# Four records instead of eight in the granule of an edge sort that scatters with accumulating DMAs

## The chip, the cores and the metric

The kernel is one program on one core of a Trainium2 chip. Its time is the device time of one execution, in microseconds (us). Of the kernel before there are three runs, 4865.23, 4868.08 and 4868.71 us, with a median of 4868.08 us. The engines are called PE (TensorE), DVE (VectorE), ACT (ScalarE), POOL (GpSimd) and SP (SyncE, which only issues transfers here).

## The reference, cut to what matters

A graph of 12,500 nodes with 256 features and 200,000 weighted edges goes through a normalised graph convolution, a linear-attention mixer and a mixture of experts. The part that matters here is the convolution's sum over the edges of each source row:

```python
xn = _layernorm(x, axis=-1)
deg = segment_sum(ew_sl, row_sl, N);  dinv = rsqrt(deg)
norm = dinv[row_sl] * ew_sl * dinv[col_sl]
msgs = (xn @ W)[col_sl] * norm[:, None]
h7 = segment_sum(msgs, row_sl, N) + b        # row_sl = src, col_sl = dst, with self-loops
x = x + mlp(h7) + mixer(xn)
x = x + ffn(layernorm(x))                    # 8 experts, top 2
```

The source of an edge is drawn uniformly, and the edges come in the order of their destinations. So the kernel first sorts them on the chip by block of 128 source rows.

## The kernel before, in words

The nodes are cut into `BLOCKS` = 98 blocks of 128 rows. The edges lie as 128 partitions by 1568 columns, and are worked through in `LOTS` = 56 lots of `LOT` = 28 columns, 3584 edges each. The program runs in phases with a barrier behind each: `setup` (constants, a histogram of blocks by lot, the places where each block's tiles start), `sort_edges` (this is where the change acts), `degrees_and_rows`, `scale_table`, `gather_and_mix`, and then the node and expert phases.

`sort_edges` writes every edge as a record of two words (8 bytes) to its place in DRAM. Records are not written one by one but in granules: `GRANULE` = 8 consecutive records, 64 bytes. Within a lot, the edges of a block form a run. A run is shifted and padded so that it begins and ends on a granule's border of the final layout. A granule that a run fills only in part holds zeros in its other records, and since the scatter adds to zeroed DRAM, lots that share a granule complete each other. Two copies of the records in DRAM (`records0`, `records1`) take the even and the odd lots, and are added up in the next phase.

How many granules a lot may need is fixed when the program is built:

```python
GROUPS_OUT = -(-(LOT * P + BLOCKS * 2 * (GRANULE - 1)) // (GRANULE * P))
SLOTS_OUT = GROUPS_OUT * GRANULE
```

That is `GROUPS_OUT` = 5 groups of 128 granules, one granule for each partition, and `SLOTS_OUT` = 40 records for each partition. One lot `n` with buffer `h` (0 or 1) does this:

- DVE, L208 (`same_block`): compares blocks, for the ranks of lot n + 1. PE, L799 and L802: turns these into ranks in PSUM. DVE, L731 and L735 to L746 (`positions`): reduces them to a place for each edge and splits the place into lane (L737, the partition), group and record within the granule.
- DVE, L750, L755 and L762 (`routes`): one-hot matrices by lane and by slot, and six products of the slot matrix with the pieces of the record's values. ACT, L711 and L716: the doubled pieces, and the comparison that says which granules lie behind each run (128 x `GROUPS_OUT`*128 elements).
- PE, L811: one small matmul for each group, which makes the shift of each granule. PE, L820: 28 matmuls that put the records into their lanes and slots.
- DVE, L769, L772 and L774 (`leave`): the granules' addresses and the finished records `sort_rec`. L772 waits until the scatters of lot n - 2, which used the same buffer, have landed.
- POOL, L696: one indirect DMA for each group, `GROUPS_OUT` in all, that adds 128 granules to DRAM at the addresses `sort_addr`; granules with an address out of bounds are dropped.

The lines of the scatter, and of the wait for its landing:

```python
pool.wait_ge(rec_done, n + 1 + ONE); pool.wait_ge(addr_done, n + 1)
for g in range(GROUPS_OUT):                                            # L694
    pool.indirect_dma_start(
        out=k.granules[h], out_offset=bass.IndirectOffsetOnAxis(addr[:, h, g:g + 1], 0),
        in_=rec[:, h, g * GRANULE:(g + 1) * GRANULE, :], ..., compute_op=ALU.add).then_inc(scattered[h], 16)
```

```python
start_after(dve, scattered[h], SCATTERS * i)                           # SCATTERS = 16 * GROUPS_OUT
dve.tensor_tensor(addr[:, h, :], moved[:, :], s.granule_col, ALU.add).then_inc(addr_done, 1)   # L772
```

The order in which each engine works through this is written out in the code: DVE takes L208, `routes`, `positions` of the next lot, `leave`; PE takes the ranks of the next lot, L811, L820. No scheduler moves anything.

Of the kernel before, what the change touches and what calls it, by code (L numbers as in the profile page):

```python
# [35 lines left out]

assert TILES >= N_EDGES // P + BLOCKS
DST_BITS = 14
GRANULE_BITS = 3
GRANULE = 1 << GRANULE_BITS  # L40
LOT = 28
LOTS = EDGE_COLS // LOT
# [171 lines left out]
def setup(k, s):  # L214
    nc, A = k.nc, k.A
    with ExitStack() as ctx:
# [86 lines left out]
        with nc.Block() as block:  # L303
# [107 lines left out]
            def _(dve):  # L411
# [63 lines left out]
                dve.tensor_scalar(odd_i[:, :], ahead_i[:, :], GRANULE - 1, None, ALU.bitwise_and).then_inc(offs, 1)  # L475
                dve.tensor_scalar(quarter_i[:, :], ahead_i[:, :], GRANULE_BITS, None, ALU.arith_shift_right).then_inc(offs, 1)
                dve.tensor_scalar(tiles[:, :], tiles_i[:, :], 1.0, None, ALU.max).then_inc(offs, 1)
# [5 lines left out]
                dve.wait_ge(offs, 12)  # L483
                dve.tensor_scalar(run4_i[:, :], run3_i[:, :], GRANULE_BITS, None, ALU.arith_shift_right).then_inc(offs, 1)
                dve.wait_ge(offs, 13)
# [154 lines left out]
def sort_edges(k, s):  # L640
# [3 lines left out]
    with ctx:  # L644
# [43 lines left out]
        with nc.Block() as block:  # L688
# [32 lines left out]
            def _(dve):  # L721
# [5 lines left out]
                def positions(n):  # L727
                    for g in range(RANK_BANKS):
# [7 lines left out]
                    dve.wait_ge(q_done, n + 1)  # L736
                    dve.tensor_scalar(lane_i[:, :], q_i[:, :], GRANULE_BITS, P - 1, ALU.arith_shift_right,  # L737
                                      ALU.bitwise_and).then_inc(split_done, 1)
                    dve.tensor_scalar(high_i[:, :], q_i[:, :], 7 + GRANULE_BITS, GRANULE_BITS, ALU.arith_shift_right,
                                      ALU.logical_shift_left).then_inc(split_done, 1)  # L740
# [1660 lines left out]
```

## Time and profile before

| | |
|---|---|
| median of three runs | 4868.08 us |
| the profiled execution | 4868.08 us, its span 4866.3 us |
| `sort_edges`, first to last scatter | 171.4 to 930.5 us of the span |
| scatters (L696) | 280, 489.3 us busy, mean 1748 ns |
| granted clock of PE in that stretch | 0.62 of full speed |

The span runs from the first to the last instruction; 1.8 us of the profiled time lie around it. The profile gives for each engine how long it was busy, for each group of instructions what its idle time before them waited for, and a timeline by engine. Whether an engine matters is read in the stretch in question. In the page's strip of 40 slices, each of 121.7 us, slices 2 to 8 are the sort. A call of POOL for an indirect DMA is a busy instruction there: it is the time in which POOL makes the descriptors, not that of the transfer.

### The profile page before, as it was taken

To read this page: it belongs to the slowest core of one execution; us is meant where nothing else is said; L and a number is where in the kernel's file an instruction comes from. 1 tells how busy PE (TensorE), PEld (TensorE's weight loads), DVE (VectorE), ACT (ScalarE), POOL (GpSimd) and SP (SyncE) were. 2 spreads that over 40 slices of the span, in tenths; PEclk is the share of its full clock that TensorE was granted. 3 is DMA by queue.
4 is the path that set the end of the run, shared out by engine and by line. 5 is a ranking of instruction groups with operands and counts; after the bars stand their busy time and mean duration, and the time that the engine had idled before them with its cause. 6 is when DMAs were issued, how large, how long until landed. Compare 5 with 4: busy or idle time off the path is not lost. (4 is left out here: it accounts for less than half of the span.)

```text
span 4866.3 us, 90967 instructions
## 1 busy us (share of the span) xinstructions
PE 3803.9 (78%) x20723; PEld 2690.7 (55%) x20723; DVE 3267.5 (67%) x8693; ACT 1133.3 (23%) x3013; POOL 2642.9 (54%) x2385
## 2 busy tenths in 40 slices
PE   7688888487588888888777777777599689999970
PEld 6344444266344444444454445454288579999970
DVE  8899999688566666666666666665244855556643
ACT  2000000033211111111000000000055545555530
POOL 0366666400577777777777777777300022236656
PEclk9566666655799999999889888887599899999985
DMA  2011111133633333333444444444732012223344
GB/s 72 2 3 3 3 3 3 34 111 100 188 112 112 112 112 111 113 111 113 127 135 135 137 134 137 135 137 123 128 95 93 22 55 69 71 81 106 105 147 140
DMA packets 330249, 453.67 MB, mean 93 GB/s; under 512 B 96328, under 2 KB 260680, under 8 KB 330185
## 3 DMA queue, kind: packets, MB, share of 16 engines
q0 software_dynamic: 139776, 273.68, 23.0%
q1 hardware_dynamic: 175513, 169.50, 10.8%
q10 hardware_dynamic: 14898, 9.77, 0.7%
q8 instruction: 25, 0.41, 0.0%
q14 instruction: 37, 0.30, 0.0%
HBM read 354.82 MB, written 98.26 MB: 93 GB/s over the span
## 5 line engine op out<-in xcount | busy, mean ns | idle before, releaser
L1309 POOL DMA_INDIRECT rows<-table,idx x1664 | 1692.0, 1017 | 507.8 <-issue 288.0
L1593 PE MATMUL ps_seg<-rows,pick 128*128 128x256 f32 x3328 | 1150.0, 448 | 470.3 <-DMA rows<-table,idx 375.6
L1495 DVE TENSOR_TENSOR acc<-acc,ps_seg 128x256 f32 x1664 | 698.7, 420 | 718.6 <-PE ps_seg L1593 576.5
L1593 PEld LDWEIGHTS ps_seg<-rows,pick 128*128 128x128 f32 x3328 | 586.6, 206 | 959.0 <-DMA rows<-table,idx 464.1
L696 POOL DMA_INDIRECT records<-sort_rec,sort_addr x280 | 489.3, 1748 | 435.3 <-DVE sort_rec L774 349.5
L1374 DVE TENSOR_SCALAR pick<-iota_row,loc,ewt 128x128 f32<-128x128 f32 x1680 | 540.5, 360 | 21.3 <-DVE loc L1370 21.2
L2129 POOL DMA_INDIRECT arena<-ffn_rows,idx x212 | 215.4, 1016 | 454.6 <-DVE idx L2215 298.2
L2273 PE MATMUL ps_h<-arena,up_now 128*128 128x128 f32 x3392 | 415.8, 276 | 0.0
L2257 PE MATMUL ps_y<-down_now,arena 128*128 128x256 f32 x1696 | 401.0, 379 | 0.0
L2273 PEld LDWEIGHTS ps_h<-arena,up_now 128*128 128x128 f32 x3392 | 398.0, 193 | 0.1
L2257 PEld LDWEIGHTS ps_y<-down_now,arena 128*128 128x128 f32 x1696 | 306.1, 190 | 32.8
L820 PE MATMUL ps_out<-acc 128*128 128x240 bf16 x1568 | 277.7, 362 | 34.4 <-DVE acc L762 32.4
L2182 ACT ACTIVATE arena<-ps_h,up_now 128x128 f32<-128x128 f32 x848 | 242.5, 369 | 213.0 <-PE ps_h L2273 213.0
L2197 DVE TENSOR_TENSOR arena<-ps_y,down_now 128x256 f32<-128x256 f32 x212 | 90.1, 425 | 296.7 <-PE ps_y L2257 296.7
L799 PE MATMUL ps_rank<-acc 128*128 128x490 bf16 x336 | 181.2, 539 | 136.6 <-DVE acc L208 136.6
L1320 ACT ACTIVATE xT<-ps_xT 128x256 f32<-128x256 f32 x196 | 75.3, 384 | 824.4 <-PE ps_xT L1525 747.3
L820 PEld LDWEIGHTS ps_out<-acc 128*128 128x128 bf16 x1568 | 201.8, 132 | 99.7 <-DVE acc L762 29.6
L1064 PE MATMUL ps_rows_tile_deg<-rows_ew,rows_at_node 128*128 (+1 forms) x1664 | 189.5, 180 | 48.9 <-DVE rows_at_node L992 42.4
L762 DVE TENSOR_TENSOR acc<-sort_in_slot,sort_piece 128x1120 bf16<-128x1120 bf16 x336 | 224.2, 738 | 1.9
L2170 ACT ACTIVATE arena<-ps_x,gb 128x128 f32<-128x128 f32 x424 | 171.4, 454 | 181.1 <-PE ps_x L2249 181.1
L1533 PE MATMUL ps_kv<-wkv,xT 128*128 128x512 f32 x392 | 208.6, 659 | 0.0
L2210 DVE COPY down_now<-down_all 128x1280 f32 x212 | 177.2, 836 | 45.0 <-DVE arena L2197 17.2
(347 smaller groups left out, 5413.4 us busy)
## 6 DMA issues: line engine op xcount, KB each, us to landing
y_rows<-arena SPq DMA_DIRECT2D x212, 128.0 KB
rows<-table,idx POOLq DMA_INDIRECT x1664
xn<-xn_dram SPq DMA_DIRECT2D x200, 128.0 KB
rows_x<-in_x SPq DMA_DIRECT2D x100, 128.0 KB
x<-in_x SPq DMA_DIRECT2D x100, 128.0 KB, 2.9
part<-part_dram SPq DMA_DIRECT2D x50, 256.0 KB
xn_dram<-acc SPq DMA_DIRECT2D x98, 128.0 KB
table<-acc SPq DMA_DIRECT2D x14, 896.0 KB
```

Source lines behind the costliest of these rows:

```text
L696: pool.indirect_dma_start(out=k.granules[h], out_offset=bass.IndirectOffsetOnAxis(addr[:, h, g:g + 1], 0), in_=rec[:, h, g * GRANULE:(g + ...
L762: dve.tensor_tensor(valued[:, h, v, :, :].rearrange("p c (s two) -> p c s two", two=2), in_slot[:, :, :].rearrange("p c (s two) -> p c s t ...
L820: last = pe.matmul(OUT, in_lane[:, h, c, :], valued[:, h, :, c, :], start=(c == 0), stop=(c == LOT - 1))
L1309: pool.indirect_dma_start(out=rows[:, t, :], out_offset=None, in_=k.table, in_offset=bass.IndirectOffsetOnAxis(idx[:, h, t:t + 1], 0), bou ...
L1374: dve.tensor_scalar(pick[:, h, t, :], k.iota_row[:, :], loc[:, h, t:t + 1], ewt[:, h, t:t + 1], ALU.is_equal, ALU.mult).then_inc(pick_done, 1)
L1495: dve.tensor_tensor(here, here, sums(u).unsqueeze(1), ALU.add).then_inc(added, 1)
L1533: pe.matmul(ps_kv[:, :], xT[:, c, :], k.wkv[:, c, :], start=(c == 0), stop=False)
L1593: pe.matmul(sums(t), pick[:, h, t, :], rows[:, t, :], start=True, stop=True).then_inc(seg_done, 1)
L2129: pool.indirect_dma_start(out=xrow[:, u, :], out_offset=None, in_=k.ffn_rows, in_offset=bass.IndirectOffsetOnAxis(idx[:, u:u + 1], 0), bou ...
L2182: act.activation(hT[:, slot, c * P:(c + 1) * P], ps_h[slot][:, c * P:(c + 1) * P], ACT.Gelu, bias=parts[slot][1][:, c:c + 1]).then_inc(gel ...
L2257: last = pe.matmul(ps_y[slot][:, 0:D], hT[:, slot, c * P:(c + 1) * P], parts[slot][2][:, c, :], start=(c == 0), stop=(c == HC - 1))
L2273: last = pe.matmul(ps_h[slot][:, c * P:(c + 1) * P], parts[slot][0][:, d, c * P:(c + 1) * P], xT[:, slot, d * P:(d + 1) * P], start=(d == ...
```

## The change

One constant: the granule holds 4 records (32 bytes) instead of 8 (64 bytes). All else follows from it.

```diff
 DST_BITS = 14
-GRANULE_BITS = 3
+GRANULE_BITS = 2
 GRANULE = 1 << GRANULE_BITS
```

`GROUPS_OUT` becomes ceil((3584 + 98*2*3) / 512) = 9 instead of ceil((3584 + 98*2*7) / 1024) = 5, and `SLOTS_OUT` becomes 36 instead of 40. The records' place in DRAM, and so all phases behind the sort, stay as they were.

On POOL, in the loop over pairs of lots of `sort_edges`, each lot's row of indirect DMAs changes (the last figures are the shape of one DMA's target and how often it is issued in a row):

```order
 L682 ISA
 L693 REGISTER_ALU
-L696 DMA records<-sort_rec,sort_addr 26624x16 x5
+L696 DMA records<-sort_rec,sort_addr 53248x8 x9
 L692 REGISTER_ALU
-L696 DMA records<-sort_rec,sort_addr 26624x16 x5
+L696 DMA records<-sort_rec,sort_addr 53248x8 x9
 L682 REGISTER_ALU
 L682 COMPARE_AND_BRANCH
```

Nothing changes its place; five DMAs of 128 x 16 words have become nine of 128 x 8 words. On DVE, in the same loop, from the end of one lot's `leave` through the next lot's `routes` (`acc` is the name of the memory that lends the sort its buffers):

```order
 L83 REGISTER_ALU
-L772 TENSOR_TENSOR sort_addr<-sort_moved,acc 128x5
-L774 TENSOR_REDUCE sort_rec<-ps_out 128x80
+L772 TENSOR_TENSOR sort_addr<-sort_moved,acc 128x9
+L774 TENSOR_REDUCE sort_rec<-ps_out 128x72
 L208 ISA
 L208 TENSOR_TENSOR acc<-acc 128x2744
 L750 TENSOR_TENSOR acc<-acc,sort_lane 128x3584
-L755 TENSOR_TENSOR sort_in_slot<-acc,sort_slot 128x1120
-L762 TENSOR_TENSOR acc<-sort_in_slot,sort_piece 128x1120 x6
+L755 TENSOR_TENSOR sort_in_slot<-acc,sort_slot 128x1008
+L762 TENSOR_TENSOR acc<-sort_in_slot,sort_piece 128x1008 x6
```

Here too the order stays, and only the widths differ.

## Rows read from the trace of the kernel before

**Rows 1.** The page's strip of 40 slices, in tenths of a slice.

```profile
DVE  8899999688566666666666666665244855556643
...
POOL 0366666400577777777777777777300022236656
```

**Rows 2.** POOL's groups: shape and count, busy us, mean ns, idle before.

```profile
L1309 POOL DMA_INDIRECT rows<-table,idx x1664 | 1692.0, 1017 | 507.8 <-issue 288.0 <-PE ps_seg L1593 213.3 <-DVE idx L1364 6.4
L696 POOL DMA_INDIRECT records<-sort_rec,sort_addr x280 | 489.3, 1748 | 435.3 <-DVE sort_rec L774 349.5 <-issue 85.9
```

**Rows 3.** DVE's timeline in one lot: start, us busy, line, operation, count.

```profile
689.07 0.41 DVE L774 TENSOR_REDUCE sort_rec<-ps_out 128x80 f32<-128x240 f32 x1 [0.36 <-PE ps_out L820]
689.39 1.58 DVE L208 TENSOR_TENSOR acc<-acc 128x2744 bf16<-128x2744 bf16 x1
690.89 2.02 DVE L750 TENSOR_TENSOR acc<-acc,sort_lane 128x3584 bf16<-128x3584 bf16 x1
692.82 0.74 DVE L755 TENSOR_TENSOR sort_in_slot<-acc,sort_slot 128x1120 bf16<-128x1120 bf16 x1
693.59 4.00 DVE L762 TENSOR_TENSOR acc<-sort_in_slot,sort_piece 128x1120 bf16<-128x1120 bf16 x6
697.51 3.33 DVE L731 TENSOR_REDUCE sort_q<-ps_rank 128x5 f32<-128x490 f32 x6
...
702.66 0.41 DVE L774 TENSOR_REDUCE sort_rec<-ps_out 128x80 f32<-128x240 f32 x1 [0.42 <-PE ps_out L820]
```

**Rows 4.** POOL's timeline in the same lot.

```profile
690.41 1.99 POOL L696 DMA_INDIRECT records<-sort_rec,sort_addr  x1 [3.71 <-DVE sort_rec L774]
692.71 1.63 POOL L696 DMA_INDIRECT records<-sort_rec,sort_addr  x1 [0.30 <-issue]
694.64 1.78 POOL L696 DMA_INDIRECT records<-sort_rec,sort_addr  x1 [0.30 <-issue]
696.72 1.65 POOL L696 DMA_INDIRECT records<-sort_rec,sort_addr  x1 [0.30 <-issue]
698.67 1.56 POOL L696 DMA_INDIRECT records<-sort_rec,sort_addr  x1 [0.31 <-issue]
703.93 2.24 POOL L696 DMA_INDIRECT records<-sort_rec,sort_addr  x1 [3.71 <-DVE sort_rec L774]
```

**Rows 5.** POOL's timeline: the sort's first two calls, and first and last of its last lot.

```profile
171.42 2.15 POOL L696 DMA_INDIRECT records<-sort_rec,sort_addr  x1 [165.52 <-DVE sort_rec L774]
173.87 2.08 POOL L696 DMA_INDIRECT records<-sort_rec,sort_addr  x1 [0.30 <-issue]
...
921.56 1.55 POOL L696 DMA_INDIRECT records<-sort_rec,sort_addr  x1 [2.61 <-DVE sort_rec L774]
...
928.99 1.55 POOL L696 DMA_INDIRECT records<-sort_rec,sort_addr  x1 [0.30 <-issue]
```

**Rows 6.** DVE's and POOL's timelines, last lot but one.

```profile
907.76 2.02 DVE L750 TENSOR_TENSOR acc<-acc,sort_lane 128x3584 bf16<-128x3584 bf16 x1
908.71 2.50 POOL L696 DMA_INDIRECT records<-sort_rec,sort_addr  x1 [3.75 <-DVE sort_rec L774]
```

**Rows 7.** Busy time in windows; the last three columns: PE clock, DMA share, GB/s.

```profile
200.00:800.00 600.00, 483.22 (x2946) 285.34 (x2943) 570.42 (x1100) 52.88 (x88) 384.12 (x221) 0.62 0.14 3
925.00:931.00 6.00, 0.00 (x0) 0.00 (x0) 0.00 (x0) 0.00 (x0) 4.66 (x3) 0.50 0.21 4
931.00:931.50 0.50, 0.00 (x0) 0.00 (x0) 0.00 (x0) 0.00 (x0) 0.00 (x0) 0.50 0.31 5
```

**Rows 8.** Issues of another indirect DMA (last: us to landing), and its calls.

```profile
arena<-y_rows,back_idx POOLq DMA_INDIRECT x98, 3.2
...
L2142 POOL DMA_INDIRECT arena<-y_rows,back_idx x98: 1005/1349/1570, 4342.3 to 4701.2; - x98
```

**Rows 9.** Timeline of the first gather, and the first matmul that needs it.

```profile
1257.56 1.11 POOL L1309 DMA_INDIRECT rows<-table,idx  x1 [0.91 <-issue]
...
1261.45 0.79 PE L1593 MATMUL ps_seg<-rows,pick 128*128 128x256 f32 x1 [1.18 <-DMA rows<-table,idx]
```

## The prediction

> **What bounds the kernel now.** The change acts in one phase, so I first looked in the strip of slices for that phase [rows 1]: slices 2 to 8, where DVE shows nines and POOL sixes. DVE is full there, POOL has room. The groups of POOL say why it is idle [rows 2]: of 435 us of idle time before the scatters, 349.5 us are waits for `sort_rec` of L774, which DVE makes; 85.9 us are "issue", a fixed gap between calls. The timeline of one lot then gives the period. DVE's L774 ends one lot at 689.07 and the next at 702.66 [rows 3], POOL's first call comes at 690.41 and then at 703.93 [rows 4]: 13.5 us. Over the whole sort the first calls of the lots are (921.56 - 171.42) / 55 = 13.64 us apart [rows 5]. In a lot DVE never rests for more than the 0.36 to 0.42 us ahead of L774 [rows 3]. POOL works from 690.41 to 700.23 and then waits 3.71 us [rows 4]. So DVE bounds the sort, with POOL at 9.8 us of 13.6, and the reader should keep the slack of 3.7 us in mind.
>
> **The change part by part.** *DVE and PE get less to do.* L755 and L762 shrink from 1120 to 1008 columns. By the two rows of the same form, 2.02 us for 3584 columns and 0.74 for 1120 [rows 3], a column costs 0.52 ns, so each of the seven instructions loses 0.06 us: 0.41 us, and L774 some 0.04. DVE alone would need about 13.15 us a lot. L769 and L772 grow by four elements in a row, and PE gets four more tiny matmuls a lot at L811 against 10% fewer columns at L820; ACT's comparison at L716 grows from 640 to 1152 columns, on an engine that is under 10% busy here (52.9 of 600 us [rows 7]). All of these stay beside other work, and I cost them at nothing.
>
> *POOL gets nine calls for five.* The question is what one call costs. The last lot shows calls with nothing beside them: 1.55 us each, 0.30 us behind the one before; from the first of five to the last, 921.56 to 928.99, it is 1.857 us from start to start [rows 5]. Does a call with half the bytes cost less? The nearest rows say that bytes don't set it: a gather of 128 x 256 words takes 1.02 us, a scatter-add of 128 x 16 words 1.55 [rows 2, 5]. Nor do granules that are dropped: a lot fills on average 3584 + 98*7 = 4270 of the 5120 places, so its fifth call has some 22 granules of 128, and still takes 1.56 us [rows 4]. I take 1.555 us + 0.30 us, nine times: 16.71 us. That alone is above DVE's 13.15: **POOL becomes the bound.** The bounds for one call are 1.02 us (the gather) and 1.75 us (the scatters' mean [rows 2]).
>
> *Calls beside DVE take longer, and that must be sized.* In the lot of [rows 4] the calls take 1.99, 1.63, 1.78, 1.65 and 1.56. Laid over DVE's rows one rule fits: a call that starts while an instruction of DVE with two SBUF inputs runs (L208, L750, L755, L762) is longer by what is left of that instruction, less 0.12 us; later ones do not matter. At 690.41 L208 has 0.56 us left: 1.555 + 0.44 = 1.99, as shown. At 692.71 L750 has 0.20 left: 1.63. At 173.87 it is 2.08 [rows 5], and in [rows 6] L750 has 1.07 us left at 908.71: 2.50. A call beside L731, which reads PSUM, stays at 1.56. So far this costs 0.83 us (8.61 - 5 * 1.555) in this lot, and 1.12 in the sort's first two calls alone [rows 5]. Here the Trainium skill has a rule (SBUF — State Buffer, "SBUF: two separate sides"): the port pair that DVE and GpSimd share is an exclusive lock, and who comes second is fully blocked until the other's instruction ends. The rows agree for the start of a call, and disagree for the rest of it: the call at 694.64 lies wholly beside L762 and loses 0.22 us.
>
> With POOL as the bound, DVE's place in the lot is set anew: L772 must wait until lot n - 2 has landed, while POOL works on n - 1. Landing behind a call's end: 3.2 us from issue less 1.35 of call = 1.85 us for one gather, 1261.45 - 1258.67 = 2.8 us at most for another, the gather's first [rows 8, 9]; for the scatter itself the transfers stop about 1 us behind the last call's end, at 931.5 [rows 7], and the receipt comes on top. L208 then starts some 0.6 us after the landing, L750, L755 and L762 behind it. I stepped nine calls through that pattern by the rule above for landings of 1.0 to 3.8 us. The calls of a lot lose 0.75 us where they start between the long instructions and up to 2.45 us where one starts just behind L750's begin, a sawtooth with a mean of 1.7; for 1.85 to 2.8 us it runs from 0.8 to 2.4. I take 1.3 us, above the 1.12 that two calls lost beside the whole row of long instructions [rows 5], and keep 0.7 and 2.5 as ends. Period: 16.7 + 1.3 = **18.0 us** (17.4 to 19.2).
>
> *What the new wait holds up.* Behind DVE's wait at L772 are L774 and the next lot's L208. They need about 13 us to come round and have 18, and the next records must be there only when POOL ends its present lot, a period later: landing (under 3) + 0.8 us is far below 18. So POOL never starves, and PE, which waits for DVE, doesn't matter either.
>
> *The transfers.* A lot's valid granules go from 534 to (3584 + 98*3)/4 = 970, of 32 bytes. With calls back to back the 16 DMA engines are 21% busy [rows 7]; per call that is 0.4 us of 1.86. There is room for more than four times the price.
>
> *The sum.* 56 lots * 18.0 = 1008.0 us, less the last 0.3 us gap and about 2 us in the last two lots, where DVE is done: 1005.7 us from the first call to the end of the last. Before it was 930.54 - 171.42 = 759.1. The first call is moved by less than 0.5 us. Difference +246.6 us; phases behind the sort get the same data in the same places. The profiled execution took 4868.08 us, the same as the median: 4868.1 + 246.6 = **5115 us**. With 17.4 us it is 5081, with 19.2 us 5182.
>
> **The rivals.** *DVE stays the bound, and the kernel is faster.* If a call's price went by the words it moves, nine calls of half the words would hide: from a call of 1.16 us down (9 * 1.46 = 13.15) POOL is off the path. Then each lot gains DVE's 0.45 us: 56 * 0.45 = 25 us, 4843 us. For it: the words of a call are halved. Against it: the gather with 16 times the words is the cheaper call [rows 2]. A call between 1.16 and 1.4 us would give 4.8 to 5.03 thousand; no row points there.
>
> *Full lock-out.* If POOL could make no descriptor while DVE runs with two SBUF inputs, a lot would be 16.7 + 8.1 = 24.8 us (L208, L750, L755, L762 as shrunk), 56 * 24.8 - 759 = +630, 5498 us. This is also how the Trainium skill's rule reads if taken for the whole call (same page, "Who interferes with whom"). The calls beside L762 in [rows 3, 4] speak against it.
>
> *The DMA engines become the bound.* If a 32-byte add into DRAM cost so much more than a 64-byte one that a call's transfers took 2.35 us instead of 0.4, the lot would be 9 * 2.35 = 21.1 us and the time 5291 us. For it: the pieces are small, and the share was 0.31 to 0.21 around the last calls. Against it: a sixfold price.
>
> **How the numbers follow.** My forecast (POOL's nine calls bound the lot, 17.4 to 19.2 us) gets 0.87; faster by hidden calls 0.03; a cheaper call with POOL still the bound 0.04; full lock-out 0.02; DMA-bound 0.04. The measurement tells 0.2% (10 us) from no change. Faster by more than that is 0.03, within it 0.01 (the period would have to land within 0.17 us of the old one), slower 0.96. For the range I take 5070 to 5190: the period's ends with some 10 us on each side, for a call price that is off by 0.02 us.
>
> **What would show it.** Right: 504 calls at L696 of 1.55 us or more with a mean near 1.70; POOL's idle time before them nearly all "issue", about 150 us, the waits for L774 gone except for the first lot and the last; POOL's slices of the sort at nines and DVE's down to seven; starts of lots 17.4 to 19.2 us apart; DVE idle ahead of L772 behind a DMA of `records`; the sort's last call ending near 1177 us; the stretches behind it of the same length as before. Wrong: calls near 1.1 us, a DMA share above 0.5 in the sort, or POOL waiting for L774 or on the landing in each lot.

## The result, and the profile after

The changed kernel takes 5127.32 us (median of four runs, 5125.0 to 5128.83) against 4866.65 us of the kernel before. The ratio is 1.0536, with a 95% interval of 1.0519 to 1.0555: 261 us slower. The forecast was 5115 us, 5070 to 5190.

The profiled execution has a span of 5122.8 us, 256.5 us above the one before. All of it lies in the sort. A mark for the sort's end is POOL's first instruction of the next phase:

```profile
1192.68 1.55 POOL L696 DMA_INDIRECT records<-sort_rec,sort_addr  x1 [0.30 <-issue]
1200.18 0.15 POOL L918 IOTA rows_tile_col_i<- 128x13 int32 x1 [5.95 <-POOLq L104]
```

In the kernel before, the timeline has this instruction here:

```profile
937.88 0.15 POOL L918 IOTA rows_tile_col_i<- 128x13 int32 x1 [7.33 <-POOLq L104]
```

It comes 262.3 us later now. What follows it takes 3922.6 us against 3928.4 before, a difference of no account. The page's strip, of the changed kernel, answers to [rows 1]: DVE has gone from nines to sixes, POOL from sixes to eights, and the sort reaches into slice 10.

```profile
DVE  8766666664866666666666666666534675556653
...
POOL 0588888882017777777777777777700012236656
```

```profile
L696 POOL DMA_INDIRECT records<-sort_rec,sort_addr x504 | 869.7, 1726 | 317.7 <-DVE sort_rec L774 164.5 <-issue 153.2
```

The row above, from POOL's groups by shape, answers to [rows 2]. There are 504 calls instead of 280, and the mean is nearly the same, 1726 ns to 1748. The idle time is 164.5 us ahead of the first call, one wait, and 153.2 us of fixed gaps: POOL waits for nobody in the sort any more. DVE does now. Its instructions at L772, in the view of one line, show what they wait for:

```profile
L772 DVE TENSOR_TENSOR sort_addr<-sort_moved,acc x56: 168/170/172, 169.1 to 1161.9; 128x9 int32<-128x9 f32 x56
...
  DMA records<-sort_rec,sort_addr: 289.1, 53
```

Now one lot. First POOL's timeline of the changed kernel; the call at 704.00 is the first of its nine, and the next lot begins at 722.20:

```profile
702.14 1.55 POOL L696 DMA_INDIRECT records<-sort_rec,sort_addr  x1 [0.30 <-issue]
704.00 1.55 POOL L696 DMA_INDIRECT records<-sort_rec,sort_addr  x1 [0.30 <-issue]
705.86 2.39 POOL L696 DMA_INDIRECT records<-sort_rec,sort_addr  x1 [0.30 <-issue]
708.55 1.63 POOL L696 DMA_INDIRECT records<-sort_rec,sort_addr  x1 [0.30 <-issue]
710.49 1.60 POOL L696 DMA_INDIRECT records<-sort_rec,sort_addr  x1 [0.30 <-issue]
712.39 2.07 POOL L696 DMA_INDIRECT records<-sort_rec,sort_addr  x1 [0.31 <-issue]
714.76 1.56 POOL L696 DMA_INDIRECT records<-sort_rec,sort_addr  x1 [0.30 <-issue]
```

And DVE's timeline beside it:

```profile
704.87 0.17 DVE L772 TENSOR_TENSOR sort_addr<-sort_moved,acc 128x9 int32<-128x9 f32 x1 [5.39 <-DMA records<-sort_rec,sort_addr]
704.95 0.38 DVE L774 TENSOR_REDUCE sort_rec<-ps_out 128x72 f32<-128x216 f32 x1
705.24 1.58 DVE L208 TENSOR_TENSOR acc<-acc 128x2744 bf16<-128x2744 bf16 x1
706.74 2.02 DVE L750 TENSOR_TENSOR acc<-acc,sort_lane 128x3584 bf16<-128x3584 bf16 x1
708.67 0.68 DVE L755 TENSOR_TENSOR sort_in_slot<-acc,sort_slot 128x1008 bf16<-128x1008 bf16 x1
709.38 3.65 DVE L762 TENSOR_TENSOR acc<-sort_in_slot,sort_piece 128x1008 bf16<-128x1008 bf16 x6
```

Three things are to be seen. The five calls of this lot that start while no two-input instruction of DVE runs (704.00, 714.76 and three more) take 1.55 or 1.56 us, with half the words of a call of before. The call at 705.86 is longer by 0.84 us: L208 had 0.96 us left, less the 0.12 us of the rule. Worked out for every call of the trace, the rule gives the length of 503 of the 504 within 0.1 us; the exception is the sort's first call, which is 0.21 us longer. And the landing is short: the lot before ends its last call at 703.69, and L772 runs at 704.87, 1.2 us later. Over all lots the starts lie 18.3 us apart, against 13.64 before.

### The profile page after: what moved, and what is told of

Its sections match the earlier page's. It is cut to its first block and busy times, and to the rows that moved or that the text cites. A ratio compares the mean times of both kernels' runs of the same rounds, so it can differ in the third digit from the quotient of the medians.

```text
span 5122.8 us, 91863 instructions
## 1 busy us (share of the span) xinstructions
PE 3792.7 (74%) x20947; PEld 2706.4 (53%) x20947; DVE 3252.1 (63%) x8693; ACT 1157.3 (23%) x3013; POOL 3019.5 (59%) x2609
## 5 line engine op out<-in xcount | busy, mean ns | idle before, releaser
L696 POOL DMA_INDIRECT records<-sort_rec,sort_addr x504 | 869.7, 1726 | 317.7 <-DVE sort_rec L774 164.5
L799 PEld LDWEIGHTS ps_rank<-acc 128*128 128x128 bf16 x336 | 35.5, 106 | 456.8 <-issue 386.9
L820 PE MATMUL ps_out<-acc 128*128 128x216 bf16 x1568 | 262.4, 358 | 14.2 <-DVE acc L762 13.4
L820 PEld LDWEIGHTS ps_out<-acc 128*128 128x128 bf16 x1568 | 211.5, 138 | 50.1 <-issue 12.5
L711 ACT ACTIVATE sort_piece<-acc 128x336 bf16 (+1 forms) x56 | 27.0, 482 | 891.1 <-DVE acc L762 878.1
```

What stands on the lines that cost most here:

```text
L696: pool.indirect_dma_start(out=k.granules[h], out_offset=bass.IndirectOffsetOnAxis(addr[:, h, g:g + 1], 0), in_=rec[:, h, g * GRANULE:(g + ...
L799: pe.matmul(ps_rank[g][:, 0:BLOCKS * len(c)], s.earlier, s.same[:, h, c.start:c.stop, :], start=True, stop=False, skip_group_check=True)
L820: last = pe.matmul(OUT, in_lane[:, h, c, :], valued[:, h, :, c, :], start=(c == 0), stop=(c == LOT - 1))
```

## The experiments

The extra time of calls beyond 1.555 us each is called lock waits below. The time of the sort is read as the stretch from POOL's first scatter to its first instruction of the next phase: 766.5 us in the kernel before (171.42 to 937.88) and 1028.8 us in the changed one (171.34 to 1200.18). The runs were made in three sets: first four empty calls, eight calls, six calls and all instructions cut in four; then one empty call, the copies on ACT and L208 moved in the changed kernel; then the rest. The kernel before took 4864.75, 5198.18 and 5204.37 us in them. The difference lies in the gather phase, whatever the kernel, and not in the sort. Totals are therefore compared with the kernel before of the same set, and across sets by the sort's stretch, which is that of one profiled execution each.

**Four empty calls added to the kernel before.** The number of calls apart from their size.

```diff
+                    for g in range(4):
+                        pool.indirect_dma_start(out=k.granules[h], out_offset=...(far[:, g:g + 1], 0),  # all out of bounds
+                            in_=rec[:, h, g * GRANULE:(g + 1) * GRANULE, :], ..., compute_op=ALU.add).then_inc(scattered[h], 16)
```

> The kernel before (granules of 8 records, five calls of 128 x 16 words a lot) with four more scatter calls in each lot whose addresses are all out of bounds, so that they move nothing. It tells the number of calls from their size. Theory (POOL's price goes by the call, 1.555 us + 0.304 us whatever it moves): nine calls a lot again, period 16.7 us + about 1.5 us of lock waits = 18.2 us, 5110 to 5140 us in all, the time of the changed kernel, though records, granules and DVE's work are those of before. Rival (the price goes by the granules or bytes that a call really moves, or small 32-byte adds cost the extra time): the empty calls are short and the time stays at 4867 to 4950 us.

Measured: 5112.87 us, ratio 1.0511 (1.0494 to 1.0529). POOL's groups by shape:

```profile
L699 POOL DMA_INDIRECT records<-sort_rec,sort_addr x280 | 505.3, 1805 | 109.6 <-issue 85.0 <-DVE sort_rec L785 24.6
L705 POOL DMA_INDIRECT records<-sort_rec,sort_far x224 | 350.6, 1565 | 68.2 <-issue 68.2
```

An empty call costs 1.565 us and its gap of 0.304, as much as a full one. Four of them bring back 248 of the 261 us though the granules are those of before. The other 13 us are in the lock waits: (855.9 - 504 * 1.555) / 56 = 1.29 us a lot here, and (869.7 - 504 * 1.555) / 56 = 1.54 us in the changed kernel. Small adds have no part in the loss that these runs can show.

**One empty call added.** The same edit with one call.

> The kernel before with one more scatter call in each lot, its addresses out of bounds. Theory (a call is free as long as POOL's calls end before DVE's next records, with 3.7 us of idle time a lot and 1.86 us a call): no change, 4862 to 4868 us, POOL's idle time before a lot's first call 1.85 us. Rival (calls slow DVE or PE, or each costs its price wherever it stands): 56 * 1.86 = 104 us more, 4970 us.

Measured: 5196.65 us against 5198.18 us of the kernel before in that set, ratio 0.9997 (0.9987 to 1.0006). POOL's timeline, a lot's first call:

```profile
692.06 1.99 POOL L699 DMA_INDIRECT records<-sort_rec,sort_addr  x1 [1.86 <-DVE sort_rec L785]
```

The idle time ahead of it is 1.86 us where [rows 4] have 3.71. A sixth call is free, as the slack said.

**Eight calls in the changed kernel.** The ninth group of granules is left out.

```diff
-        SCATTERS = 16 * GROUPS_OUT
+        CALLS = 8
+        SCATTERS = 16 * CALLS
...
-                    for g in range(GROUPS_OUT):
+                    for g in range(CALLS):
```

> The changed kernel with eight instead of nine scatter calls a lot; the ninth group of granules, in which hardly any granule is used (970 of 1152 a lot on average), is left out. Theory (POOL bounds by the number of calls): 1.86 us less a lot, period 16.4 us, 56 * 1.86 = 104 us less, 5023 us. Rival (the transfers or their landing bound the lot): what moves is the same, so the time stays within 10 us of 5127 us.

Measured: 5033.94 us, ratio 1.035 (1.0333 to 1.0367), 93 us less than the changed kernel; the sort takes 934.8 us, 94.0 less. The rival with the transfers as the bound falls, since that group hardly carries anything. Of the 10 us short of 104, 7 lie in lock waits: the calls are busy for 789.3 us, so (789.3 - 448 * 1.555) / 56 = 1.65 us a lot against 1.54, 56 * 0.12. The other 3.4 lie behind the last call, where POOL waits 9.36 us for the next phase instead of 5.95. Records that come late cost nothing: the 21 waits for L774 behind the first one stand where the fixed gap would, and POOL's idle time in the sort is 17.0 us less than in the changed kernel (300.7 against 317.7), which is 56 gaps.

**Six calls in the changed kernel.** Groups seven to nine are left out.

> The changed kernel with six scatter calls a lot; groups seven to nine of the granules are left out, so about a fifth of the records never reach DRAM. Theory: POOL needs 6 * 1.86 + 1.2 = 12.3 us a lot and DVE about 13.15, so DVE bounds again, with its 0.45 us a lot less than in the kernel before: period 13.2 us, 56 * 0.45 = 25 us below the kernel before, 4842 us (4835 to 4855). Rival (each call beyond the number is paid whatever DVE does, as if POOL's and DVE's times added up): 3 * 104 = 312 us below 5127 and no floor, 4815 us; or, if DVE's narrower instructions bring nothing, 4867 us.

Measured: 5008.71 us, ratio 1.0296 (1.0279 to 1.0314). As a total this is far from all that was expected, and it can't be used: the sort does what the theory said, and a later phase is disturbed by the missing records. The sort's stretch is 172.8 to 921.90 = 749.1 us, 17 us below the kernel before (forecast 25). The time comes back in the gather, whose rows POOL fetches by the records' contents:

```profile
L1310 POOL DMA_INDIRECT rows<-table,idx x1664 | 1684.1, 1012 | 673.0 <-PE ps_seg L1594 362.2 <-issue 295.1 <-DVE idx L1365 15.7
```

Its idle time is 673 us against 508 in [rows 2]. Missing records read as zeros, so many gathers would go for the same row; that this is what slows them is not shown, as it was not tried by itself. The lesson for the method is that work may be left out only where nothing later depends on its values.

**All two-input instructions of DVE cut in four.** Each of L208, L750, L755 and L762 becomes four instructions of 7 columns of edges.

```diff
+                        for c in range(0, LOT, 7):
+                            last = dve.tensor_tensor(valued[:, h, v, c:c + 7, :]..., in_slot[:, c:c + 7, :]..., piece2[...], ALU.mult)
```

> The changed kernel with each of DVE's instructions with two SBUF inputs in the sort's loop (L208, L750, L755, L762) cut into four of 7 columns of edges each: the same work, about 2.1 us more of DVE time a lot, which hides behind POOL. Theory (a call is held at its start until the one DVE instruction that runs then ends): what is left of an instruction is shorter, the waits of a lot fall from 1.54 us to 1.0 to 1.2 us, 20 to 30 us in all: 5097 to 5107 us. Rival (calls are slowed in proportion to the time that DVE works beside them): the waits grow with DVE's time from 7.7 to 9.8 us a lot, by 0.4 us, 5150 us.

Measured: 5225.76 us, ratio 1.0748 (1.073 to 1.0766), 98 us above the changed kernel, 90 of them in the sort (1118.7 us against 1028.8). A clear miss, in the other direction: the lock waits are 3.14 us a lot. The timeline of POOL and DVE shows where they come from; in this kernel L762 is the comparison that was L755, and L771 the products that were L762:

```profile
700.55 0.88 DVE L762 TENSOR_TENSOR sort_in_slot<-acc,sort_slot 128x252 bf16<-128x252 bf16 x4
700.76 1.69 POOL L700 DMA_INDIRECT records<-sort_rec,sort_addr  x1 [0.30 <-issue]
701.47 4.89 DVE L771 TENSOR_TENSOR acc<-sort_in_slot,sort_piece 128x252 bf16<-128x252 bf16 x24
702.76 5.03 POOL L700 DMA_INDIRECT records<-sort_rec,sort_addr  x1 [0.30 <-issue]
```

The call at 702.76 takes 5.03 us. The 24 short products end at 706.36, so it waited for all that was left of the row, 3.60 us less 0.12, and not for the piece that ran. In the trace, 55 of the 65 calls that start within such a row were held to its end, within 0.02 us. But the calls at 697.01 and 700.76, beside the pieces of L208 and L755, took only 1.58 and 1.69 us. The second of them started with 0.67 us of its row left, and its pieces are as short as those of the products (0.28 us). Of 24 calls that started at the second of these four pieces, 23 waited for no more than the one piece. So short pieces alone do not hold a call.

**The changed kernel once more, in the third set.** No edit.

> The changed kernel itself, to have it on the same chip as the others of this call: 5.2 to 5.6% above the kernel before, 255 to 290 us, whatever the chip's own level, since the sort doesn't depend on it.

Measured: 5458.92 us against 5204.37 us, ratio 1.0493 (1.0475 to 1.0512). The difference is 255 us against 261 in the first set, at the lower end of what was expected; the ratio is below the expected 5.2 to 5.6% since the rest of the program is longer there. The sort takes 1028.8 us in both sets.

**Only the long ones cut.** L208 and L750 in four, L755 and L762 whole.

```diff
-                        same_block(dve, s, 1 - h, n + 1).then_inc(same_done, 1)
+                        same_block(dve, s, 1 - h, n + 1, 4).then_inc(same_done, 1)      # 4 pieces of 7 columns
+                    for c in range(0, LOT, 7):
+                        last = dve.tensor_tensor(in_lane[:, h, c:c + 7, :]..., pairs(s.iota_b)..., lane2[:, c:c + 7, :]..., ALU.is_equal)
```

> The changed kernel with only DVE's long comparisons L208 and L750 cut in four (pieces of about 0.51 and 0.62 us), L755 and L762 whole. Theory (a call waits for what is left of the instruction that runs, as long as the pieces are of this length; the held call of 5 us in the kernel with all of them cut came from the 24 pieces of 0.28 us at L762): waits of 1.35 to 1.5 us a lot instead of 1.54, 2 to 12 us less than the changed kernel on the same chip, no call above 3.3 us. Rival (any cut run of two-input instructions locks POOL out to its end): waits above 3 us a lot, 80 us or more above the changed kernel.

Measured: 5416.18 us, ratio 1.0415 (1.0397 to 1.0434). So cutting the long ones brings 43 us (49 in the sort, 980.4 us against 1028.8), where 2 to 12 were expected. POOL's groups:

```profile
L700 POOL DMA_INDIRECT records<-sort_rec,sort_addr x504 | 821.2, 1629 | 315.6 <-DVE sort_rec L780 163.0 <-issue 152.6
```

The waits fall to (821.2 - 504 * 1.555) / 56 = 0.67 us a lot, from 1.54; 56 * 0.87 = 49 us. The second call of a lot, the one that met L208, takes 1.77 us in this kernel. Without the row of 24 short products there are no calls of 5 us, so that row is what kept them out before. But the rule doesn't hold here as it did. In 44 calls that start within 0.04 us of the beginning of a piece of L750, or of the first product of L762, there is no wait at all, and the instruction of DVE is 0.04 to 0.07 us longer; by the rule these calls would have lost 25 us, which is more than half of the 43. And two calls beside the pieces of L750 (0.62 us) take 3.70 us, past the end of their row, where no call above 3.3 us was expected. What decides between one piece, the whole row and no wait stays open.

**L208 moved ahead of the wait, changed kernel.** The same instructions in another order; the comparison for lot 1 goes ahead of the loop.

```diff
                 def body(n, h, i, more):
-                    if more:
-                        same_block(dve, s, 1 - h, n + 1).then_inc(same_done, 1)
                     routes(n, h)
                     if more:
                         positions(n + 1)
+                    if more and not (isinstance(n, int) and n == LOTS - 2):
+                        same_block(dve, s, h, n + 2).then_inc(same_done, 1)
                     leave(n, h, i)
```

> The changed kernel with DVE's comparison L208 for the next lot ahead of the wait for the landed scatter (L772) instead of behind L774. The same work in another order; DVE is idle 5 us a lot ahead of that wait. Theory (POOL bounds; a call waits for what is left of DVE's two-input instruction at its start): L750 now starts where L208 did, 1.24 us behind a lot's first call, so the second call waits for 2.02 - 0.74 = 1.28 us of it instead of 0.85, the third for 0.64 us of L762; with L208 elsewhere some 0 to 0.3 us more: waits of 1.9 to 2.3 us a lot instead of 1.54, 5147 to 5170 us. Rival (waits go by how long DVE works beside POOL): no change, 5127 us. Rival (DVE still matters for the lot): faster than 5127 by up to 56 * 1.5 = 84 us, since L208 leaves the chain behind the landing.

Measured: 5489.66 us, ratio 1.0559 (1.0543 to 1.0575). The changed kernel was not run in this set, so the sort's stretch decides: 1058.0 us against 1028.8, 29 us more. (The totals, across two sets, differ by 30.7 us.) POOL's second and third call of a lot and DVE's L750:

```profile
702.12 2.03 DVE L750 TENSOR_TENSOR acc<-acc,sort_lane 128x3584 bf16<-128x3584 bf16 x1
```

```profile
702.71 2.86 POOL L696 DMA_INDIRECT records<-sort_rec,sort_addr  x1 [0.30 <-issue]
705.87 1.60 POOL L696 DMA_INDIRECT records<-sort_rec,sort_addr  x1 [0.31 <-issue]
```

The second call waits for 2.86 - 1.555 = 1.30 us; 1.28 was expected. The lock waits are 2.06 us a lot, within the 1.9 to 2.3 expected. With as much DVE work as ever, its place alone costs 29 us, and taking 1.6 us out of what follows the landing gains nothing. Both rivals fall: DVE's amount of work doesn't set the waits, and DVE isn't on the path.

**The kernel before: what bounds it?** First the two doubled copies (L744, L746) on ACT; the edit shows the first of them.

```diff
-                    dve.tensor_copy(lane2[:, :, :], lane_i[:, :].unsqueeze(2).to_broadcast([P, LOT, 2])).then_inc(lane2_done, 1)
+                    act.wait_ge(split_done, 3 * n + 3)
+                    act.activation(lane2[:, :, :], lane_i[:, :].unsqueeze(2).to_broadcast([P, LOT, 2]), ACT.Copy).then_inc(lane2_done, 1)
```

> The kernel before with the two doubled copies of lane and slot (L744, L746) on ACT instead of DVE. DVE starts them 0.10 and 0.12 us ahead of what follows. Theory (DVE alone sets the period of the kernel before, POOL has 3.7 us of slack and ACT is nearly idle): 0.2 us less a lot, 56 * 0.2 = 12 us less, 4852 us (4848 to 4858). Rival (the wait for PE ahead of L774, 0.36 to 0.42 us a lot, is what ends last, so DVE's saving only lengthens that wait): 4864 us, no change.

Measured: ratio 0.9999 (0.999 to 1.0008), no change. The view of L774 in that kernel says why:

```profile
  PE ps_out L829: 38.4, 56
```

This is DVE's wait ahead of its last instruction of the lot. It is 38.4 us in 56 lots, against 27.1 us (the same view of the kernel before): the 11.3 us that DVE saved turned into waiting. So in the kernel before, the lot's end is set by DVE's L762 and PE's 28 matmuls of L820 behind it, not by DVE alone as I had written.

**The kernel before with L208 ahead of the leaving lot.** The edit shown above, on granules of eight.

> The kernel before (granules of 8, five calls) with DVE's comparison L208 for the next lot ahead of L769, L772 and L774 instead of behind. Theory (in the kernel before, PE's L820 ends last ahead of L774 and DVE idles 0.36 to 0.42 us a lot for it; L208 fills that time): the wait for PE goes, the period falls by about 0.4 us, 56 * 0.4 = 22 us less than the kernel before on the same chip. Rival (POOL is late next: its first call comes 1.5 us later in DVE's order): POOL has 3.7 us of slack, so a gain of less than 5 us would speak for it.

**And with both edits.**

> The kernel before with both edits: L208 ahead of the leaving lot, and the two doubled copies on ACT. Theory: with the wait for PE gone, what leaves DVE now counts: 22 us + 56 * 0.22 = 12 us, 34 us less than the kernel before. Rival (PE still ends last): no more than the 22 us of the one edit.

Measured: L208 moved alone, 5189.13 us against 5204.37 us of the kernel before in that set, ratio 0.9973 (0.9964 to 0.9983), 15 us less; both edits, 5169.99 us, ratio 0.9936 (0.9922 to 0.9949), 34 us less. These are small differences, but both intervals lie below 1. The sort's stretches are 746.4 and 735.1 us, 20 and 31 us below 766.5; 22 and 34 were expected. The wait for PE ahead of L774 is gone from all lots but two, and now the copies count. The last kernel beats both the one before and the changed one. It doesn't need the change.

## Why the prediction was right, point by point

*POOL becomes the bound.* Right. Nine calls at 1.555 us and a gap of 0.304 us are 16.73 us of the measured 18.3 us a lot; a call's price depends neither on its words nor on whether its granules land, which the four empty calls show by themselves. The rival of a cheaper call falls with them, and so does the full lock-out, which asked for 24.8 us a lot.

*The lock waits.* The rule read from a few calls of before held for all but one of the changed kernel's (0.84 us in the lot above, and 1.30 us in the reordered kernel, both within 0.02 us). That it is DVE's instruction which holds the call is borne out by the reordered kernel; the two kernels with cut instructions show that the rule is not the whole of it.

The term that was mis-sized is the sum of these waits. I took 56 * 1.3 us less 2 us for the last two lots, 70.8 us; measured are 869.7 - 504 * 1.555 = 86.0 us, 15.2 more. With 2.0 us for the gap (0.304 for 0.300) the stretch from the first call to the end of the last is 1022.9 us, 17.2 above the 1005.7 of the sum. A shorter wait behind the last call (5.95 us for 7.33) gives 1.4 back, hence 262.3 us against 246.6. I had the landing at 1.85 to 2.8 us, from gathers; it is 1.2 us for the scatter. At 1.2 us the second call starts in L208 and the lot loses 2.39 + 1.63 + 1.60 + 2.07 - 4 * 1.555 = 1.47 us, as the rows above show. So the rule was right, but the landings that I held likely (1.85 to 2.8 us, with losses of 0.8 to 2.4) leave out the true one, and the 1.3 us was a choice within a wide range: that it came within 0.24 us of the measured value is in part luck. The nearer row was the one that shows the transfers stopping about 1 us behind the last call [rows 7], and I gave it too little weight.

Of the Trainium skill's rule (SBUF — State Buffer, "SBUF: two separate sides") this trace bears out the exclusion at the start of a call, and the held call of 5.03 us shows it for a whole row of instructions. It doesn't bear out the exclusion for the rest of a call: the call at 705.86 has 1.43 us to run when L208 ends, L750 runs beside it, and neither is longer for it (L750 takes 2.02 us as in [rows 3]).

*The transfers.* Right that they don't bound: the DMA share of the sort is 0.18, and leaving out a nearly empty group saves as much as a call costs.

*DVE and PE get less to do.* The price was a little high: six calls show a sort 17 us shorter than before, not 25. One thing was put at nothing: in that kernel and in the changed one DVE's L746 and L769, just ahead of L772, take 0.48 and 0.38 us in the mean, against 0.19 and 0.17 in the kernel before, where POOL is idle at that point. That POOL's calls are the cause was not tried. "DVE bounds the sort" was incomplete, since PE's L820 was last ahead of L774; the forecast did not depend on it.

*The rest of the program.* Right, 3922.6 us against 3928.4.

## What to carry to other kernels

Where a queue issues fixed-price calls, count calls and not bytes: halving the piece nearly doubled the calls (5 to 9), and the 3.7 us of slack that hid one more call could not hide four. When the bound moves to another engine, that engine's price must be taken as it will be there, beside everything else, with the phase that the new wait sets. And before moving work off the engine that looks full, see what its last instruction waits for: the same edit was worth nothing while that wait stood, and 11 us of the sort (746.4 to 735.1) once it was gone.

## What the runs showed of the hardware

- A scatter call takes 1.55 us alone, full or with every address out of bounds (1.565 us mean), for 8 or for 16 words a partition; a gather call of 256 words takes 1.0 us.
- In the kernel before and the changed one, a call that starts beside a two-input bf16 instruction of DVE (0.68 to 2.02 us long) waits for what is left of it less 0.12 us, in all calls but the first. A row of 24 pieces of 0.28 us mostly held a call to its end (55 of 65, one call of 5.03 us); four pieces of the same length did not (23 of 24).
- The increment of a scatter-add to DRAM reached the waiting engine 1.2 us behind the end of its call.
- The same kernel took 4865 us in the first set and 5198 and 5204 us in the later ones, 7% more, none of it in the sort (1028.8 us in the changed kernel in the first and in the third set). The gather phase has it. It can't be put down to the chip: the record has the sets on chips 5, 11 and 5, the same number for the first set and for the third. These are windows over the gather, of the kernel before in the first set and of the kernel with one empty call in the second:

```profile
1256.00:3460.00 2204.00, 1736.71 (x6076) 1046.61 (x6076) 1433.48 (x4440) 274.31 (x687) 1692.50 (x1668) 0.90 0.44 122
```

```profile
1256.00:3800.00 2544.00, 1735.01 (x6094) 1189.15 (x6094) 1424.98 (x4458) 263.53 (x687) 1706.65 (x1669) 0.80 0.39 106
```

The matmuls are as busy in both (1736.7 and 1735.0 us), the mean granted clock of PE is 0.90 and 0.80, and 340 us more pass. Longer fetches don't show as the cause: ahead of its matmuls on the fetched rows, PE's waits for them are 375.6 us in the first and 13.2 us in the second. Whether the lower clock is the cause, these runs don't tell.
